# Transposing the second norm's rows with VectorE out of DRAM, running the gate two batches behind, and taking the first norm's statistics on ScalarE

## The reference: gated cross attention, then a mixture of experts

```
x = x + tanh(g_xattn) * softmax(layernorm(x) @ Wq @ K.T / sqrt(512)) @ V     # K, V = ctx @ Wkv
n = layernorm(x)
probs = softmax(n @ gate_w + gate_b, over the 256 tokens of a batch)          # 8 experts
two best experts of each token, with their probabilities
v[e] = sum over tokens that chose e of prob * relu(mlp_e(n))                  # three layers of 512
out  = x + tanh(g_ffn) * sum of v[e] over the token's two experts
```

## Time and profile before

| what | value |
|---|---|
| median of 3 runs | 930.74 us (929.98 to 931.37) |
| the profiled execution's own time | 929.86 us |
| its span in the trace | 928.1 us, clock 0.988 of full speed in the mean |
| busy share of the span: PE, PEld | 98%, 92% |
| busy share: DVE, ACT, POOL | 75%, 54%, 30% |
| first stage, one turn of the loop | 19.95 us, with PE busy in all of it |
| second stage from 450 us on | PE busy 464.27 of 470 us |

### The profile page before, as it was taken

The page is one execution under the profiler, slowest core; times in us unless marked ns, Lnnn a source line. Parts: engine busy times, 40 slices in busy tenths (PEclk is TensorE's granted clock), DMA queues, the critical chain, the costliest instruction groups (busy, mean ns, idle before and its releaser), DMA issues.

```text
span 928.1 us, 18701 instructions
## 1 busy us (share of the span) xinstructions
PE 909.5 (98%) x5746; PEld 858.4 (92%) x5746; DVE 694.9 (75%) x1305; ACT 503.5 (54%) x707; POOL 276.2 (30%) x314
## 2 busy tenths in 40 slices
PE   8999999999999999999999999999999999999985
PEld 6989988888988888999999999999999999999981
DVE  6667767777767877967777777777777777777756
ACT  5355444455444368556666666666666666666521
POOL 4224454444444557742111111111111111110003
PEclk9999999999999999999999999999999999999995
DMA  7423332223232355457766888853753753752009
GB/s 239 159 105 124 104 124 91 91 91 136 95 108 69 88 158 122 133 145 211 187 197 167 247 251 245 247 177 109 185 170 111 192 167 111 191 169 64 18 16 362
DMA packets 91924, 138.67 MB, mean 149 GB/s; under 512 B 28528, under 2 KB 56944, under 8 KB 88688
## 3 DMA queue, kind: packets, MB, share of 16 engines
q1 hardware_dynamic: 84464, 120.86, 42.4%
q0 software_dynamic: 7424, 17.38, 7.2%
HBM read 106.66 MB, written 31.53 MB: 149 GB/s over the span
## 4 chain that ended last, share of the span: by engine, by line
PE 91%; DVE 3%; issue 1%; POOL 1%; DMA 1%; SPq 1%; ACT 1%; DVEq 0%; POOLq 0%; ACTq 0%
PE bank L1339 28%; PE bank L1341 28%; PE bank L1340 28%; DVE x_all L1329 2%; PE bank L1353 1%; PE bank L1422 1%; PE bank L1463 1%; PE bank L1465 1%; DMA idx<-slot_pair 0%; POOL slot_pair L633 0%; DMA wk_raw<-in_wk_t 0%; PE bank L1373 0%; PE bank L1479 0%; PE bank L1606 0%; PE bank L1414 0%
## 5 line engine op out<-in xcount | busy, mean ns | idle before, releaser
L1339 PE MATMUL bank<-h_hi,w_hi 128*128 128x352 f32 x744 | 241.4, 324 | 0.0
L1341 PE MATMUL bank<-h_hi,w_lo 128*128 128x352 f32 x744 | 240.1, 323 | 0.0
L1340 PE MATMUL bank<-h_lo,w_hi 128*128 128x352 f32 x744 | 239.0, 321 | 0.0
L663 POOL DMA_INDIRECT xg<-xn_dram,idx x72 | 93.0, 1291 | 359.3 <-DMA idx<-slot_pair 343.6
L952 DVE TENSOR_TENSOR w_lo<-w_raw,w_hi 128x2048 fp32r<-128x2048 f32 (+1 forms) x74 | 166.5, 2250 | 23.8 <-ACT w_hi L824 18.7
L841 ACT ACTIVATE h<-bank,bias 128x352 f32<-128x352 f32 x192 | 95.8, 551 | 139.8 <-PE bank L1341 114.6
L824 ACT ACTIVATE w_hi<-w_raw 128x2048 fp32r<-128x2048 f32 x71 | 135.5, 1908 | 35.5 <-PE bank L1341 33.1
L952 DVE TENSOR_TENSOR h_lo<-h,h_hi 128x704 fp32r<-128x704 f32 x88 | 78.1, 888 | 83.9 <-ACT h_hi L847 83.9
L1339 PEld LDWEIGHTS bank<-h_hi,w_hi 128*128 128x128 f32 x744 | 139.8, 188 | 0.1
L1340 PEld LDWEIGHTS bank<-h_lo,w_hi 128*128 128x128 f32 x744 | 139.8, 188 | 0.0
L1341 PEld LDWEIGHTS bank<-h_hi,w_lo 128*128 128x128 f32 x744 | 139.3, 187 | 0.0
(11 more groups left out here) (218 smaller groups left out, 1721.4 us busy)
## 6 DMA issues: line engine op xcount, KB each, us to landing
w_raw<-in_w SPq DMA_DIRECT2D x24, 1024.0 KB, 5.4
xq<-rows_dram SPq DMA_DIRECT2D x80, 176.0 KB
w_raw<-in_w SPq DMA_DIRECT2D x48, 256.0 KB
rows_dram<-xg SPq DMA_DIRECT2D x20, 512.0 KB, 3.3
wb<-slot_pair SPq DMA_DIRECT2D x24, 352.0 KB
xt_raw<-in_x_t SPq DMA_DIRECT2D x16, 512.0 KB, 3.9
c_raw<-in_ctx_t SPq DMA_DIRECT2D x16, 512.0 KB
x_all<-in_x SPq DMA_DIRECT2D x16, 512.0 KB
```

What stands on the lines that cost most here:

```text
L663: pool.indirect_dma_start(xg[0:n, c], None, rows, bass.IndirectOffsetOnAxis(ap=idx[0:n, c, 0:1], axis=0)).then_inc(gathered, 16)
L1339: pe.matmul(out_ap, lh, rh, start=(i == 0), stop=False)
L1340: pe.matmul(out_ap, lh, rl, start=False, stop=False)
L1341: last = pe.matmul(out_ap, ll, rh, start=False, stop=(i == n - 1))
```

## The change

For batches 0 to 9 (`GATE_BLOCKS = 10`) PE no longer transposes `xn2`. SP reads the stored rows back from `xn2_dram` in four DMAs of 32 partitions each (`load_gate_rows`), DVE turns the 32x32 blocks in one instruction (`gate_blocks`, inside `attended`, between the residual sum and the second norm's statistics), ACT makes `gt_hi` in one copy and DVE `gt_lo` in one subtraction a turn later. The gate of batches 0 to 10 (`LATE_GATE = 11`) runs two turns behind in place of one: `gate_logits(b-2)` between `values` and `pt_transposes`, `gate_transposes(b-2)` after `x_times_a`, `ranks(b-2)` in the middle of `p_times_v`. Batches 11 to 15 keep a gate one turn behind, and batches 10 to 15 their PE transposes, which now read every fourth column, since the gate's weights are laid out for that order of the features. `gw_raw` is loaded by four DMAs for the same reason.

The first norm's statistics of all batches move from DVE to ACT: a copy with a running sum for the mean, and a square with the mean as bias and a running sum for the variance. POOL computes the mean between the two and takes `context_low` ahead of `norm1_scale`. The loop covers batches 3 to 10; 11 to 14 are written out.

```diff
-BATCHES = (-1, 3, B - 3, B - 1)
+BATCHES = (-1, 3, 11, B - 1)
+GATE_BLOCKS = 10
+LATE_GATE = GATE_BLOCKS + 1
+def by_dve(m):
+    return not isinstance(m, int) or 0 <= m < GATE_BLOCKS
+def late(m):
+    return not isinstance(m, int) or 0 <= m < LATE_GATE
+def in_time(m):
+    return isinstance(m, int) and LATE_GATE <= m < B
+def by_pe(m):
+    return isinstance(m, int) and GATE_BLOCKS <= m < B
...
-            sp.dma_start(gw_raw[:], gate_w).then_inc(s_small, 16)
+            for q in range(NQ):
+                sp.dma_start(gw_raw[q * QB:(q + 1) * QB], gate_w[:, q].rearrange("(i k) e -> i k e", k=DC)).then_inc(s_small, 16)
...
+            def load_gate_rows(m):
+                need(sp, xn2_out, 16 * (m + 1))
+                need(sp, gt_ready, m)
+                for q in range(NQ):
+                    rows = xn2_dram[bass.ds(m * S, S), q * P:(q + 1) * P].rearrange("(g b) d -> b g d", b=QB)
+                    sp.dma_start(gate_rows[q * QB:(q + 1) * QB], rows).then_inc(gate_rows_in, 16)
...
+                if by_dve(b - 1):
+                    load_gate_rows(b - 1)
...
+            def norm1_mean(m):
+                need(pool, ln1_sum, RC * (m + 1))
+                need(pool, ln1_stat, RC * m)
+                wait_alone(pool, "pool")
+                pool.tensor_scalar(mean1[:], sum1[:], -1.0 / D, None, ALU.mult).then_inc(ln1_mean, 1)
...
                 elif exists(b + 1, B):
+                    norm1_mean(b + 1)
+                    context_low(b + 1)
                     norm1_scale(b + 1)
-                    context_low(b + 1)
...
+            def gt_high_late(m):
+                need(act, gate_done, m)
+                act.wait_ge(gt_ready, m + 1)
+                act.activation(gt_hi[:], gt_raw[:], ACT.Copy).then_inc(gt_his, 2)
...
+            def norm1_sum(m):
+                need(act, x_in, 16 * (m + 1))
+                need(act, ln1_mean, m)
+                need(act, ln1_stat, RC * m)
+                wait_alone(act, "act")
+                for c in range(RC):
+                    act.activation(unread[:, c], x_all[:, bass.ds(m, 1), c].rearrange("p a d -> p (a d)"), ACT.Copy,
+                                   accum_out=sum1[:, c:c + 1]).then_inc(ln1_sum, 1)
+
+            def norm1_squares(m):
+                act.wait_ge(ln1_mean, m + 1)
+                need(act, ln1_small, 4 * m)
+                wait_alone(act, "act")
+                for c in range(RC):
+                    act.activation(unread[:, c], x_all[:, bass.ds(m, 1), c].rearrange("p a d -> p (a d)"), ACT.Square,
+                                   bias=mean1[:, c:c + 1], accum_out=square1[:, c:c + 1]).then_inc(ln1_stat, 1)
...
+                if late(b - 2):
+                    gate_low(b - 2)
+                    pt_high(b)
                 if exists(b + 1, B) and not (isinstance(b, int) and b == BATCHES[0]):
                     context_high(b + 1)
...
+                if late(b - 2):
+                    gate_exp(b - 2)
                 if exists(b + 1, B):
+                    if late(b - 2):
+                        norm1_sum(b + 1)
+                    else:
+                        norm1_squares(b + 1)
                     qa_high(b + 1)
...
                 if exists(b + 2, B):
                     xt_high(b + 2)
+                if exists(b + 1, B) and late(b - 2):
+                    norm1_squares(b + 1)
...
+            def gate_blocks(m):
+                dve.wait_ge(gate_rows_in, 16 * NQ * (m + 1))
+                need(dve, gt_his, 2 * m)
+                dve.transpose(gt_raw[:].rearrange("p k (g b) -> p g k b", b=QB),
+                              gate_rows[:].rearrange("p g (i k) -> p g k i", k=DC)).then_inc(gt_ready, 1)
+
+            def gt_low_late(m):
+                dve.wait_ge(gt_his, 2 * (m + 1))
+                dve.tensor_tensor(gt_lo[:], gt_raw[:], gt_hi[:].bitcast(F32), ALU.subtract).then_inc(gt_los, 2)
...
+                if by_dve(m - 1):
+                    gate_blocks(m - 1)
                 dve.wait_ge(x2_done, 2 * m + 2)
                 need(dve, ln2_small, 4 * m)
-                stats(m, st2, mv2, ln2_stat, bn_before(m, False))
+                stats(m, st2, mv2, ln2_stat, RC * m)
...
+                if late(b - 2):
+                    gate_scale(b - 2)
+                    qa_low(b + 1, [0])
+                    two_best(b - 2)
+                    qa_low(b + 1, [1])
+                    slots(b - 2, parity)
...
-                                            src[:, c, dc * P:(dc + 1) * P], ident[:])
+                                            src[:, c, dc::DC], ident[:])
...
+                if late(b - 2):
+                    gate_logits(b - 2)
                 if exists(b, B):
                     pt_transposes(b)
-                if exists(b - 1, B):
+                if by_pe(b - 1):
                     xn2_transposes(b - 1)
...
+                if late(b - 2):
+                    gate_transposes(b - 2)
...
-                    p_times_v(b)
+                    p_times_v(b, (lambda: ranks(b - 2)) if late(b - 2) else None)
```

More of the change, by code:

```diff
@@ L800, in batch @@
                     xt_high(b + 2)
+                if exists(b + 1, B) and late(b - 2):
+                    norm1_squares(b + 1)
+                if in_time(b - 1) and late(b - 2):
+                    gate_low(b - 1)
+                    gate_exp(b - 1)
             for n in range(DC):
@@ L1009, in slots, with qa_low @@
                 dve.tensor_copy(both[:, :, :, 1].bitcast(F32), top[:, :, 0:TOPK]).then_inc(slot_step, 1)
-            def qa_low(m):
+            def qa_low(m, halves=range(2)):
                 if isinstance(m, int) and m == 0:
@@ L1019, in qa_low @@
                     return
-                for k in range(2):
+                for k in halves:
                     need(dve, qa_his, 2 * m + k + 1)
@@ L1079, in batch @@
                         xt_low(b + 1)
-                    norm1_stats(b + 1)
+                if isinstance(b, int) and b - 2 == LATE_GATE:
+                    two_best(b - 2)
                 if exists(b, B):
-                    v_pt_low(b)
-                if exists(b - 1, B):
+                    v_low(b)
+                if late(b - 2):
+                    gate_maximum(b - 2)
+                if exists(b, B):
+                    pt_low(b)
+                if by_pe(b - 1):
                     gt_low(b - 1)
-                if exists(b - 2, B):
+                if in_time(b - 2):
                     slots(b - 2, parity)
-                if exists(b + 1, B):
+                if late(b - 2):
+                    gate_scale(b - 2)
+                    qa_low(b + 1, [0])
+                    two_best(b - 2)
+                    qa_low(b + 1, [1])
+                    slots(b - 2, parity)
+                elif exists(b + 1, B):
                     qa_low(b + 1)
-                if exists(b - 1, B):
+                if in_time(b - 1) and not late(b - 2):
                     gate_softmax(b - 1)
@@ L1092, in batch @@
                     attended(b)
+                if in_time(b - 1) and late(b - 2):
+                    gate_softmax(b - 1)
             def link(ins, done, step):
@@ L1431, in xn2_transposes, with x_times_a @@
                 transpose_rows(xn2, gate_banks(m), tg_done)
-            def x_times_a(m):
+            def x_times_a(m, between=None):
                 need(pe, xt_los, m + 1)
@@ L1449, in x_times_a @@
                 for n in range(DC):
+                    if n == DC - 1 and between is not None:
+                        between()
                     split_product(bQ[n // 2][:, (n % 2) * S:(n % 2 + 1) * S], cols(a_hi, a_lo, n * P, P),
@@ L1466, in gate_logits, with p_times_v @@
                 last.then_inc(gate_done, 1)
-            def p_times_v(m):
+            def p_times_v(m, between=None):
                 need(pe, pt_los, m + 1)
@@ L1471, in p_times_v @@
                 for c in range(RC):
+                    if c == RC - 1 and between is not None:
+                        between()
                     split_product(bV[c][:], cols(pt_hi, pt_lo, c * P, P), cols(v_hi, v_lo, 0, D), pv_done)
@@ L1478, in gate_transposes @@
                 for c in range(RC):
-                    last = pe.transpose(R_PROB[:, c * E:(c + 1) * E], probs[:, c * P:(c + 1) * P],
-                                        ident[0:E, 0:E])
+                    rows = slice(c, None, RC) if by_dve(m) else slice(c * P, (c + 1) * P)
+                    last = pe.transpose(R_PROB[:, c * E:(c + 1) * E], probs[:, rows], ident[0:E, 0:E])
                 last.then_inc(pt8_done, 1)
```

83 lines of the change are left out of this document (52 added, 31 removed).

## The result

The changed kernel takes 940.07 us (median of 3 runs, 938.74 to 940.12) against 930.74: the ratio is 1.0098, with a 95% interval of 1.0085 to 1.0112. Forecast were 924.7 us and, eight times in ten, no more than 930.5. The profiled execution's span is 937.0 us in place of 928.1.

What follows compares the result with a forecast made beforehand. PE was taken to bound the first stage, busy in all 19.95 us of a turn. Terms -8.7 + 0.7 + 1.65 + 0.3 = -6.05 on the profiled 929.86 gave 923.8, as run median 924.7 us; range 921.0 to 930.5.

Steps and rivals of the forecast that it cites:

- I cost the round trips at nothing: Dependency loops across DVE, POOL and ACT fit into PE's shorter turn: no cost, up to 0.5 us a turn above.
- Removed transposes, -8.7: On PE, dropping eight transposes a batch saves 0.87 us each batch, 8.7 for ten batches.
- Nothing is added to PE's list: On PE, the gate's products, its small transposes and ranks only change places: no added work.
- Strided transposes, +0.7: On PE, batches 10 to 15 transpose with a stride of four elements: 0.12 us a batch dearer, 0.7 for six.
- The block transpose, 2.0: On DVE, the new transpose of 1024 elements a row takes 2.0 us, between 1.3 and 2.75.
- ACT's passes, 0.6 and 0.7 net: On ACT, each 512-element sum takes 0.6 us and each square 0.7, 2.6 a batch.
- No second table load: Rival on ACT: the square needs another activation table, two loads a turn of 1.28 us each, 965 us; chance 0.02.
- DMA: The four row reads arrive 18 us into the turn, at worst 24; DVE asks at 21.5: usually 3 us of cover.
- The first round trip, 18.1: From one two_best to the next through DVE, POOL and ACT: 18.1 us, 18.4 with hops, against 19.1 of PE.
- The second round trip: From the end of x_times_a through norm1_scale, sends and qa_lo: 19.2 us against 19.6 allowed, 0.4 to spare.
- The wait at `ranks`, 0.15, at worst 0.4: PE waits 0.15 us for DVE's two_best in each of eleven late turns, +1.65; at worst 0.4 a turn.
- slower: ACT's list delays `qa_hi`: Rival: late qa_hi delays two_best, ranks and the next turn; 20.3 us a turn, 935 us in all; chance 0.10.

Runs made afterwards that it cites:

- experiment 14: Changed kernel with norm2_scale before the sends (except turns of batches 13, 14), statistics before block transposes, transposes into PSUM; 925.82 us, 0.9948 of the kernel before.
- experiment 1: Changed kernel with the block transpose written to PSUM in place of SBUF, gt_hi made in two halves; 932.49 us, ratio 1.0022 to the kernel before.
- experiments 9: Changed kernel with norm2_scale before the sends (except the turn of batch 14), statistics before block transposes, transposes into PSUM; 928.67 us, 0.9988 of the kernel before.
- experiment 5: Changed kernel with ACT's two summing passes moved from in front of qa_high to between its halves; 945.11 us, ratio 1.0160 to the kernel before.
- experiments 10: Changed kernel with ACT's summing passes between the halves of qa_high and POOL's context_low as four instructions of a quarter each; 935.73 us.

## Why the prediction was wrong

The step that failed is "I cost the round trips at nothing, with up to 0.5 a turn above". The first trip was put at 18.1 (18.4 with hops) against 19.1 of PE, and it measured 20.95. Two of its terms were mis-sized, `norm2_scale` by 1.57 and `two_best` by 0.71, because small operations of one engine were held to the end of a long instruction of the other. The duration of each operation had been read where it had other neighbours than it would have in the new turn.

Point by point:

- **Removed transposes, -8.7.** Right as a price: turn 1 is shorter by 1.84, which is 0.87 and the gate products that have moved on (0.94 to 0.97).
- **"Nothing is added to PE's list".** Not quite. From start to start of the groups, turn 3 of experiment 14 (19.29) against turn 8 of before (19.94): the stretch of `pt_transposes` and `xn2_transposes` falls by 0.93, but `p_times_v`, now with `ranks` in its middle, goes from 2.78 to 3.04, the gate's small transposes from 0.21 to 0.32, `x_times_a` from 5.84 to 5.93; `scores` and `values` are 0.20 shorter. So 0.65 of the 0.93 is left, as in turn 2 of the changed kernel (19.29). That this comes so near to the forecast 19.2 is in part luck: the wait of 0.15 in that sum did not come in turn 2, and the changed places cost about as much.
- **Strided transposes, +0.7.** Right: turn 14 has the list of before but for the stride, and is 20.04 in place of 19.94; 0.12 was forecast.
- **The block transpose, 2.0.** Right: 2.02 to 2.07 in ten instructions. It was DVE's busy time only; its output in SBUF was the part with a price.
- **ACT's passes, 0.6 and 0.7 net.** Right: 0.615 and 0.708 and a read of 0.185, most of which lies under the next pass; 1.23 for the two sums. No second table load: that rival falls.
- **DMA.** Right: the rows were always there before DVE asked.
- **The first round trip, 18.1.** Measured from turn 8 to turn 9, from `two_best` at 199.84 to `two_best` at 220.79, 20.95. `norm2_scale` was put at 1.76 and is 3.33 (+1.57); `two_best` was put at 1.16 and is 1.87 (+0.71); everything else, thirteen terms, was put at 15.2 and is 15.75. Without the two holds the trip would be 18.7, an estimate from these terms, which PE's turn would cover; in every second turn of experiment 1, 19.54 long, it does.
- **The second round trip.** It did not decide: the last operation of `norm1_scale` ended at 204.02, 5.2 after the end of `x_times_a` (5.4 in the sum), and POOL's first send then waited for DVE's `pair`, that is, for the first trip.
- **The wait at `ranks`, 0.15, at worst 0.4.** 1.07 to 1.76 where it occurs. DVE could not finish `two_best` in 1.16. In experiments 9 and 14, where `oh` is at 0.19 to 0.31, no wait at `ranks` reaches 0.2 in turns 2 to 10, and the turn is 19.28 to 19.52.
- **The rival "slower: ACT's list delays `qa_hi`", 935.** The direction was right and the mechanism not: it asked for an error of 1.25 in rows that lay back to back, and the error came from POOL and DVE, whose rows did not lie so any more. Its sum also left out the three turns 11 to 13, where PE waited 0.65 and 0.73 for the second norm before its own transposes; they came out 3.8 us longer, 0.9 of it the gate products put off in turn 1.
- **Fetches, +0.3.** No run shows this term. Turn 0 of the changed kernel begins at 27.01, that of the kernel before at 27.24.
- **The ends of the ranges.** 0.5 in each of eleven turns on 924.7 is 930.2 and not 930.5, 0.4 in ten is 928.7 and not 928.5, and 0.7 in ten turns is 931.7 and not the 930.7 of "no change". The result lies far outside either way.

The Trainium skill, SBUF — State Buffer, section "SBUF: two separate sides", states the rule that would have given this: VectorE and GpSimd share one pair of ports, held whole by whichever begins first, for the length of its instruction, when the VectorE operation runs in its two-port mode, or takes both its operands from SBUF beside a GpSimd operation that reads SBUF. The traces agree with it: 0.2 becomes 1.0 beside 1.22 of `xt_lo`, `oh` ends within 0.1 of `context_low`, quarters shorten the hold to a quarter, and `gt_low` with an operand in PSUM leaves L668 at 0.23. `probs`, one tensor operand, fits its two-port mode; no run shows the mode itself. The prediction read the durations of `gt_lo`, `xt_lo`, `context_low` and `norm2_scale` and never asked which pairs would overlap in the new turn.

**How the forecast's number stands.** Experiment 14 does all that the change does, in another order and with the transposed rows in PSUM, and has 925.8. That is 4.7 faster than the kernel before, where 6.05 were forecast: most of the gain summed up for PE was there. It needed an order in which neither the sends nor the block transposes lie between two instances of `two_best`. Its turn 15 begins at 315.32, 4.9 before that of the kernel before: 1.84 + 0.66 + 0.66 + 7 x 0.45 = 6.3 from turns 1 to 10, 0.3 from the start, less 1.7 in turns 11 to 14, 0.9 of it the products put off.

One thing stays open: what the new order would give the kernel before by itself was not tried. Its turn was all PE, so there is little for it to take there, but that is an argument and no run.

The turn is 19.28 in turns 2 and 3 of experiment 14 and about 19.50 from turn 4 on, and PE counts as busy in all of it in both. The rows show where most of the 0.2 lies: between the last product of `values` and the first one of the gate. In turn 3 their starts are 0.22 apart, in turn 8 0.39:

```profile
86.19 0.39 PE L1464 MATMUL bank<-wv_hi,c_lo 128*128 128x512 f32 x1
86.41 0.28 PE L1586 MATMUL bank<-gt_hi,gw 128*40 128x256 f32 x1
...
183.48 0.39 PE L1464 MATMUL bank<-wv_hi,c_lo 128*128 128x512 f32 x1
183.87 0.31 PE L1586 MATMUL bank<-gt_hi,gw 128*40 128x256 f32 x1
...
182.44 1.29 DVE L1051 TENSOR_TENSOR gt_lo<-bank,gt_hi 128x512 fp32r<-128x512 f32 x2
```

`gt_lo`, which the gate's products wait for, ends at 183.73 in turn 8, 0.14 ahead of them, and in turn 3 0.4 ahead. So PE's turn still holds a short wait for `gt_lo`, hidden by the modelled length of the product before it. This is read from the rows; no run takes it out.

## What to carry to other kernels

When work moves between engines or in time, write down for the new turn which VectorE operations on SBUF will lie beside which GpSimd operations, not only how long each is; a small operation of 0.2 us can cost nearly the whole of its neighbour (2.25 beside 2.36). A round trip that fits by 0.4 us has no reserve against one such meeting, and shortening it may make the meeting worse: take the long links out of it by order (the four sends here), or give one of the two a PSUM operand. Before giving up a change that came out slower, look whether the engine that it was to relieve is idle: the gain may be there and be waiting.

## What was unexpected in the hardware

- Operations of 2 and 32 elements a row took 1.0 and up to 2.25 us beside an instruction of the other engine of 1.22 and 2.36 us, and ended within 0.1 us of it (turn 9; turn 7 of experiment 5).
- The hold follows the instruction, not the bytes: the same 1024 elements in four instructions held `oh` for 0.4 and `ind` for 0.5 where one instruction had held `oh` for up to 2.1 us (experiments 10 and 5), at a price of 2.81 in place of 2.39 us for themselves.
- The first norm's sums and squares on ACT cost 0.615 and 0.708 us for 512 elements with 0.185 us for the read, and the block transpose 2.03 us for 1024 elements a row, 1.98 ns each.
